# A decoder layer on one core: the value matmuls of the last cross-attention bursts are issued in halves of a burst instead of step by step

## The reference, cut to what matters

```python
att = einsum('bhqd,bhkd->bhqk', q, k) * scale          # 512 x 512, causal
y = einsum('bhqk,bhkd->bhqd', softmax(att), v)
attc = einsum('bhqd,bhkd->bhqk', qc, kc) * scale       # 512 x 1024
y = y + einsum('bhqk,bhkd->bhqd', softmax(attc), vc)
return y @ Wp + bp
```

## Time and profile before

| what | value |
|---|---|
| median of 3 runs | 2311.99 us |
| the profiled execution, whole | 2316.21 us |
| its span, first to last instruction | 2314.5 us |
| mean granted TensorE clock | 0.962 of full |
| PE busy | 2157.3 us (93%) |
| DVE busy | 1869.3 us (81%) |
| ACT busy | 1384.9 us (60%) |

### The profile page before, as it was taken

One profiled execution on the slowest core, in us unless ns is written; L12 is line 12 of the kernel. 1 busy time (PEld: TensorE's weight loads), 2 busy tenths in 40 slices (PEclk: granted clock), 3 DMA queues, 4 the chain that ended last, 5 costly groups with the idle time before them and its releaser, 6 DMA issues.

```text
span 2314.5 us, 37338 instructions
## 1 busy us (share of the span) xinstructions
PE 2157.3 (93%) x12965; PEld 977.6 (42%) x12965; DVE 1869.3 (81%) x5137; ACT 1384.9 (60%) x2977; POOL 189.1 (8%) x349
## 2 busy tenths in 40 slices
PE   5999999999989999899999999999998999979992
PEld 2344434543345434454335543454334543335432
DVE  5858869788878879788797887978888787978854
ACT  2934687456854579446784468745686456844560
POOL 3011001000011000110001100110001100001000
PEclk7899999999999999999999999999999999999995
DMA  3600034000520006100160002400043000510000
GB/s 106 133 10 1 1 65 82 10 1 1 112 44 11 1 19 119 21 8 1 36 120 10 2 1 63 93 10 1 1 86 61 10 1 10 102 36 1 1 10 9
DMA packets 250844, 81.67 MB, mean 35 GB/s; under 512 B 236064, under 2 KB 247328, under 8 KB 250656
## 3 DMA queue, kind: packets, MB, share of 16 engines
q1 hardware_dynamic: 250656, 79.29, 16.7%
HBM read 16.35 MB, written 4.19 MB: 9 GB/s over the span
## 4 chain that ended last, share of the span: by engine, by line
PE 79%; DVE 10%; ACT 6%; issue 3%; DMA 1%; SPq 0%; POOL 0%; DVEq 0%; POOLq 0%; ACTq 0%
PE bank L1513 23%; PE bank L1566 13%; PE bank L1551 7%; PE bank L1204 7%; PE bank L1509 5%; PE bank L1470 5%; PE bank L1548 4%; DVE work L770 4%; ACT work L603 3%; PE bank L1333 3%; PE bank L1320 2%; PE bank L1526 2%; PE bank L1578 2%; PE bank L1356 1%; PE bank L1436 1%
## 5 line engine op out<-in xcount | busy, mean ns | idle before, releaser
L659 ACT ACTIVATE work<-bank 128x512 f32<-128x512 f32 (+3 forms) x1536 | 739.8, 550 | 534.1 <-PE bank L1548 268.1
L1033 DVE TENSOR_REDUCE top_half<-bank 128x1 f32<-128x512 f32 x1024 | 625.7, 682 | 25.8 <-PE bank L1513 25.8
L1513 PE MATMUL bank<-k_c,q_c 32*128 32x512 f32 x2048 | 631.3, 638 | 0.0
L1551 PE MATMUL bank<-q_c,k_c 32*128 32x512 f32 x2048 | 526.2, 633 | 0.0
L603 ACT ACTIVATE work<-work,neg 128x512 bf16<-128x512 bf16 x512 | 362.6, 715 | 30.6 <-DVE work L770 29.8
L1513 PEld LDWEIGHTS bank<-k_c,q_c 32*128 32x128 f32 x2048 | 274.8, 186 | 243.7 <-DVE top_half L1033 158.9
L770 DVE TENSOR_SCALAR_CACHE_REDUCE work<-bank 128x512 bf16<-128x512 f32 x512 | 322.4, 686 | 44.0 <-PE bank L1302 33.6
L1566 PE MATMUL bank<-work,v_flat 128*32 128x512 f32 (+3 forms) x3072 | 321.8, 544 | 5.5 <-ACT work L659 5.0
L1030 DVE CUSTOM_DVE_ANT_0 masked<-bank,mask_w 128x384 bf16<-128x384 f32 (+3 forms) x512 | 223.8, 488 | 87.9 <-PE bank L1509 82.5
L1548 PE MATMUL bank<-q_s,k_s 32*128 32x512 f32 (+3 forms) x1024 | 260.5, 480 | 0.0
L1551 PEld LDWEIGHTS bank<-q_c,k_c 32*128 32x128 f32 x2048 | 218.4, 183 | 78.4 <-ACT work L659 48.6
(11 more groups left out here) (194 smaller groups left out, 2188.8 us busy)
## 6 DMA issues: line engine op xcount, KB each, us to landing
xT_pad<-xT SPq DMA_DIRECT2D x16, 256.0 KB, 3.3
ctx_sb<-ctxT SPq DMA_DIRECT2D x8, 512.0 KB, 3.3
x_res<-x SPq DMA_DIRECT2D x8, 512.0 KB, 4.6
out<-r_sb SPq DMA_DIRECT2D x8, 512.0 KB, 3.1
work<-work SPq DMA_TRANSPOSE x112, 4.4
qk_sb<-qkT SPq DMA_DIRECT2D x1, 512.0 KB, 4.7
pe_sb<-pe_w SPq DMA_DIRECT2D x1, 256.0 KB, 3.9
v_sb<-vT SPq DMA_DIRECT2D x1, 256.0 KB, 6.5
```

The costliest lines, as they stand in the source:

```text
L659: nc.scalar.activation(pT[:, s % PT_SLOTS, g, q0:S], exp_bank(n)[:, 0:S - q0], ACT.Exp, scale=SCALE).then_inc(pT_ready, 1)
L1033: nc.vector.tensor_reduce(top_half[:, i % 2, g, u // 2, u % 2:u % 2 + 1], scores, AX.X, ALU.max, negate=True).then_inc(slot_out, 1)
L1513: mm(dst, q_c[rows, i, P * t:P * (t + 1)], k_c[rows, i, S * half:S * (half + 1)], start=True, stop=True, tile_position=(GW * g, 0)).then_i ...
L1551: mm(dst, k_c[rows, i, P * u:P * (u + 1)], q_c[rows, i, :], start=True, stop=True, tile_position=(GW * g, 0)).then_inc(sT_mm, 1)
```

## The change

The constants `SINGLES_FROM` and `SINGLES_BEHIND` go; `HALVES_FROM = 9` comes. From burst 9 on, PE multiplies two steps at a time. For bursts 9 and 10 the first half (steps 36, 37 and 40, 41) stands between the second and third head of step 39 and 43, the second half (38, 39 and 42, 43) between the second and third head of step 41 and 45. For burst 11 the first half (44, 45) stands after the scores of step 46, the second half (46, 47) after the first scores of the next batch. `pv` waits for the exponentials of the last of its steps. The instructions, their shapes and their number are the same; so are ACT's and DVE's programs.

```diff
-    SINGLES_FROM, SINGLES_BEHIND = 9, 2
+    HALVES_FROM = 9
@@ outputs_ready (DVE)
-            return [j] if s % BURST == (0 if j < SINGLES_FROM else SINGLES_BEHIND - 1) and j >= 0 else []
+            return [j] if s % BURST == (0 if j < HALVES_FROM else 1) and j >= 0 else []
@@ slot_uses
-                order.extend(("pv", j) for j in outputs_ready(s))
+                order.extend(("pv", j) for j in burst_behind(s))
@@ PE
-                def pv_step(s):
-                    pv(s // BURST, range(s % BURST, s % BURST + 1))
+                FIRST_HALF, SECOND_HALF = range(BURST // 2), range(BURST // 2, BURST)
...
                         scoresT(s, g)
-                        if g == GH - 1 and s - SINGLES_BEHIND >= BURST * SINGLES_FROM:
-                            pv_step(s - SINGLES_BEHIND)
+                        if g == 1 and s % BURST == 3 and HALVES_FROM <= s // BURST < LAST_BURST:
+                            pv(s // BURST, FIRST_HALF)
+                        if g == 1 and s % BURST == 1 and s // BURST > HALVES_FROM:
+                            pv(s // BURST - 1, SECOND_HALF)
                     for j in burst_behind(s):
-                        if j < SINGLES_FROM:
+                        if j < HALVES_FROM:
                             pv(j)
                     for part in rows_behind(s):
                         max_rows(*part)
+                    if s == ALL_STEPS - 2:
+                        pv(LAST_BURST, FIRST_HALF)
                     for part in outputs_behind(s):
                         o_transpose(*part)
-                pv_step(ALL_STEPS - 2)
                 if ahead:
...
                         first_scores(b + 1, 0, t)
-                pv_step(ALL_STEPS - 1)
+                pv(LAST_BURST, SECOND_HALF)
```

## The result

The changed kernel took 2343.9 us (median of four runs, 2342.0 to 2348.82; two more executions took 2342.77 and 2356.2). The kernel before had a fourth run of 2319.8 us in this comparison, which makes its median 2314.1. The ratio is 1.014, with a 95% interval of 1.0105 to 1.0176: slower by 24 to 41 us. The forecast was 23.6 us, a ratio of 1.0102: the right sign, inside the second interval, just under the first. As a time, 2343.9 us lies 8.3 us over the forecast's 2335.6, 0.9 us above the range that the forecast gave for its own case (2326 to 2343) and inside the whole range (2324 to 2346).

What follows compares the result with a forecast made beforehand. PE and ACT, coupled by six score banks, bound steps 37 to 47. Losses of 11.75 us (batches 1 to 5), 6.8 (0 and 6) and 5.0 (7) sum to 23.6: 2311.99 + 23.6 = 2335.6 us, range 2324 to 2346.

Steps and rivals of the forecast that it cites:

- its own case: Main forecast for the whole kernel: slower, 2335.6 us, range 2326 to 2343, chance 0.78.
- the whole range: Whole kernel: 2324 to 2346 us, holding the forecast and the start of the clock case.
- What bounds the stretch: Steps 37 to 47: PE and ACT coupled by six score banks; ACT's idle 3.43 us before, 6.5 after.
- The unit costs: Batch 3's times for scores, exponentials and value blocks, carried through steps 37 to 47: two-step cycle 5.26 us against 4.4.
- One unit cost: PE's scores: two heads in the same row group are 0.85 us apart.
- A count: Late part, per batch: eleven steps of values stood in 11 blocks; now there are 6.
- The stall on DVE: Before step 40's values, PE waits for DVE's late copy of burst 9; 1.07 us goes in five batches.
- Fewer mode changes: Rival, late value blocks: fewer changes of tiling mode save PE time, 19.4 us in all, 2292.6 us; chance 0.07.
- the 1.75 us a batch: PE's saving in late value blocks: about 0.35 us a block, 5 blocks.
- Passed on in full: End of batch: burst 11's copy comes 2.35 us later, delaying the next attention with nothing absorbed; at most 1.1 us could be.
- The clock: Rival, steps 37 to 47: PE's waits at batch end lower the clock, 13.7 us on top, 2349 us; chance 0.08.

Runs made afterwards that it cites:

- the second interval: The changed kernel measured again, unchanged, against the kernel before: 2342.67 us, 1.0111 (1.0094 to 1.0128).
- x4: Kernel before, with five score banks instead of six in the late steps, value blocks still of one step: 2327.89 us, 1.006.
- x8: Kernel before, with DVE's convolution for the batch after next moved behind the copy of burst 9: 2304.07 us, 0.9966.
- x3: Changed kernel, with bursts 9 and 10 multiplied whole and burst 11 in halves: 2346.43 us, 1.0134 to the kernel before.
- x6: Changed kernel, with exponentials of steps 37 to 47 on half of the columns: 2319.22 us, 1.0034 to the kernel before.
- x7: Changed kernel, with four matmuls on constants ahead of the last value block in batches 0 to 6: 2339.55 us, 1.0111 to the kernel before.
- x9: Kernel before, with convolution behind burst 9's copy and the next batch's first scores ahead of step 46's values: 2293.81 us, 0.9907.
- x5: Kernel before, with exponentials of steps 37 to 47 on half of the columns: 2302.81 us, 0.9977.

## Why the prediction was right, and where it was not

- **What bounds the stretch: right.** Idle ACT was counted as 6.5 us after, 6.59 was measured, though two of its six pieces were 0.62 and 0.67 us and not over 1. The unit costs carried through gave 29.1 us of exponentials (28.93), a cycle of 5.26 us (5.20), 31.9 us of stretch (31.81), the copy of burst 11 31.2 us after the start (30.98). x4 shows the coupling by itself.
- **One unit cost rested on the wrong row.** The 0.85 us between two heads of a row group was read from 16 instructions in 3.41 us. Those are 8 heads, 1.7 us of work, and half of the 3.41 is a wait for the exponentials of step 37. The value holds all the same: in the changed kernel six heads without such a wait last 1.99 us (the row at 1144.22) against 1.14 for four, so 0.85 us for the second head in a row group. Here luck helped.
- **A count.** The values of steps 36 to 47 are twelve steps, not eleven; the 11 blocks before, the 6 now and the five saved are right.
- **The stall on DVE: right.** PE's wait was for the copy of burst 9, and went with the change; x8 removes it alone.
- **Fewer mode changes: a saving that was paid back.** Blocks of 0.99 us for one step and 1.86 for two agree with what the prediction takes from the Trainium skill, "TensorEngine Tiling (Array Packing)", Tiling Modes, Key Properties, that a change of mode drains the engine. No run isolates the 1.75 us a batch, and x3 and x6 show that neither fewer changes still nor a shorter exponential turns it into a gain.
- **Passed on in full: right as far as can be told**, by the shortest parts between stretches, 244.5 us before and 244.3 after.
- **The clock: the step that failed.** It stood in the sum at zero, and as a rival at 1.7 us a batch with a chance of 0.08, on the ground that this stretch was at 1.00 with 21.2 of 22.2 us busy. I had worked out the waits at the batch's end (first scores held for banks, last block gated, in batch 7 with nothing to cover it) but had not asked what these waits do to the clock; the busy share of the stretch before said nothing of it. A fall cost 1.35 to 1.9 us, so the size was right, and it came in 5 of 8 batches in one profile and 2 of 8 in the other: 8.2 and 3.3 us in the stretches. The failed step is this term, put at nothing for waits that the prediction itself had found.
- **What the 8.3 us between 2335.6 and 2343.9 are made of.** The profiled pair accounts for 2.9: the stretches without the clock came 1.0 us under the forecast (22.6 against 23.6), the clock added 8.2 in them, and the rest of the execution gave 4.3 back. The rest, about 5.3, is scatter: the profiled execution before took 4.2 us more than the median on which the forecast stands, and the profiled one after 1.1 us less than its own median. That the clock's 8.2 us and the whole miss are about equal is chance; against the kernel before's median of 2314.1 in the same comparison the loss is 29.8 us, 6.2 more than forecast.

What stays open: which batches fall, and why the parts between the stretches take 244 us in one batch and 248 or more in the next. They go with the time at the lower clock there, but no run here isolates a rule. Nor is it known whether a fall at the end of the stretch is one more or stands in for one that would have come later.

## What to carry to other kernels

Where two engines hand work over through a ring of buffers, compare the length of the producer's longest side job with the consumer's stock (buffers times the consumer's time for one): six heads of 0.52 us don't cover 1.86 + 1.05 + 1.21 us, and every microsecond short is idle, however well the side job is packed. A merged row of matmuls that lasts longer than its count is a hidden wait. Before the price of a change is closed, look for new waits of PE at its seams: they can cost a fall of the clock on top. A few matmuls on constants kept the clock up at that place, in 23 of 23 stretches, but in x7 the whole kernel was no faster for it. And a wait that the profile puts down to an engine that had long been done belongs to another; here naming it gave the edit of x8, 0.3% faster than the kernel before, and the first of the two edits of x9, 0.9% faster.

## What the runs showed of the hardware that I had not expected

ACT starving through a whole stretch, 4.7 us of it against 2.3 to 3.4 (x4), left the clock at its upper level in all eight batches, while it fell to the lower one in 14 of 32 stretches in which PE waited 0.32 + 0.59 us, or 2.19 us in batch 7, ahead of one block, and in three of five in which it waited 1.98 us in the middle (x5). The last block then took 2.99 or 3.38 us instead of 1.92. And runs of one kernel go with the clock: in the changed kernel the run of 2342.0 us had a mean granted clock of 0.961, that of 2348.8 us 0.956 and that of 2356.2 us 0.955, while the stretches at the full clock were equal to 0.01 us within its two profiles.
